# The second transposes of each binding part moved behind the part's weighted sums, in a four-layer transformer stack on one core

## What is computed

```python
x = x + attn_a(layernorm(x), qkvw, qkvb, ow, ob)
x = x + ffn(layernorm(x), weight, bias, centroids, assignments)
x = x + attn_b(layernorm(x), bv_q, bv_k, bv_v)
x = x + ffn(layernorm(x), weight, bias, centroids, assignments)

# attn_b: 4 heads of 256
scores = einsum('bthd,bshd->bhts', xh * q_bind, xh * k_bind) * scale
attn = where(causal, sigmoid(scores * 4.0), 0.0)
out = einsum('bhts,bshd->bthd', attn, xh * v_bind)

# ffn: x is (4096, 1024)
dots = softmax(x @ centroids.T / 0.1)
hits = dots > 0.01
out = where(any(hits, 1)[:, None] & any(hits, 0)[assignments][None, :], x @ weight.T + bias, 0)
```

## Time and profile before

| | |
|---|---|
| median of 3 runs | 3347.74 us (3346.71 to 3348.81) |
| the profiled execution, own time | 3343.6 us |
| its span in the trace | 3341.8 us |
| granted TensorE clock, mean over the span | 0.989 |
| TensorE busy | 3146.8 us (94%) |
| VectorE busy | 2271.2 us (68%) |
| GpSimd busy | 1940.3 us (58%) |
| ScalarE busy | 1744.6 us (52%) |
| first scores of steps 3 and 4 | 2647.66 and 2728.91 us |

### The profile page before, as it was taken

One profiled execution on the slowest core, in us unless ns is written; L12 is line 12 of the kernel. 1 busy time (PEld: TensorE's weight loads), 2 busy tenths in 40 slices (PEclk: granted clock), 3 DMA queues, 4 the chain that ended last, 5 costly groups with the idle time before them and its releaser, 6 DMA issues. The chain is left out here.

```text
span 3341.8 us, 62425 instructions
## 1 busy us (share of the span) xinstructions
PE 3146.8 (94%) x24128; PEld 1707.6 (51%) x24128; DVE 2271.2 (68%) x3919; ACT 1744.6 (52%) x2123; POOL 1940.3 (58%) x2065
## 2 busy tenths in 40 slices
PE   0899999999999999999989799998999999999999
PEld 0355555555555555555544455554455665655444
DVE  8377777777777777777877687776466666652622
ACT  3277777777777777777667522222245555552000
POOL 2277777777777777777666522221466666641522
PEclk9999999999999999999999899999999999999999
DMA  4122222222222222222334654453222323223643
GB/s 189 41 62 71 65 71 68 71 65 72 68 78 64 71 71 65 73 66 65 109 111 127 197 166 158 152 165 118 97 83 102 104 106 107 103 76 126 219 155 145
DMA packets 277927, 344.11 MB, mean 103 GB/s; under 512 B 92289, under 2 KB 206977, under 8 KB 276610
## 3 DMA queue, kind: packets, MB, share of 16 engines
q1 hardware_dynamic: 272962, 323.33, 30.6%
q10 hardware_dynamic: 4608, 16.78, 1.3%
q0 software_dynamic: 64, 0.01, 0.0%
HBM read 200.95 MB, written 138.55 MB: 102 GB/s over the span
## 5 line engine op out<-in xcount | busy, mean ns | idle before, releaser
L734 DVE TENSOR_REDUCE nmax<-ring_ps 128x1 f32<-128x512 f32 x1024 | 677.4, 687 | 417.0 <-PE ring_ps L535 414.5
L858 POOL TENSOR_TENSOR elo<-e,ehi 128x1024 f16<-128x1024 f32 x256 | 670.1, 2618 | 354.5 <-ACT ehi L671 354.5
L665 ACT ACTIVATE e<-st_ps,exp_scale 128x1024 f32<-128x1024 f32 x512 | 571.3, 1116 | 368.7 <-PE st_ps L545 307.6
L584 PE MATMUL proj_ps<-xnT,arena 128*128 128x512 f16 x3072 | 748.9, 380 | 3.3 <-DVE xnT L779 2.5
L671 ACT ACTIVATE ehi<-st_ps,exp_scale 128x1024 f16<-128x1024 f32 x512 | 569.0, 1111 | 0.0
L1587 PE MATMUL f_ps<-wT,fxT 128*128 128x512 f16 x1920 | 433.9, 381 | 2.9 <-DMA fxT<-xT_scratch 2.9
L584 PEld LDWEIGHTS proj_ps<-xnT,arena 128*128 128x128 f16 x3072 | 272.0, 97 | 285.9 <-ACT stage L683 11.8
L535 PE MATMUL ring_ps<-ks,qs 96*128 96x512 f16 x1024 | 396.0, 387 | 16.9 <-DVE nmax L734 16.1
L545 PE MATMUL st_ps<-qs,ks 98*128 98x512 f16 x1024 | 392.3, 383 | 12.5 <-ACT ehi L671 11.2
L562 PEld LDWEIGHTS ctx_ps<-v_sb,ehi 128*128 128x128 f16 x4096 | 312.2, 97 | 153.1 <-DVE sums L761 37.7
L562 PE MATMUL ctx_ps<-v_sb,ehi 128*128 128x65 f16 x4096 | 371.7, 192 | 13.3 <-DVE sums L761 11.8
(11 more groups left out here) (233 smaller groups left out, 4658.6 us busy)
## 6 DMA issues: line engine op xcount, KB each, us to landing
qk_scratch<-qk_hl SPq DMA_DIRECT2D x128, 256.0 KB, 2.3
fxT<-xT_scratch SPq DMA_DIRECT2D x64, 512.0 KB, 3.5
qs<-qk_scratch SPq DMA_DIRECT2D x192, 128.0 KB, 2.7
ks<-qk_scratch SPq DMA_DIRECT2D x192, 128.0 KB, 2.9
arena<-x_scratch SPq DMA_DIRECT2D x48, 512.0 KB, 4.4
ctx_scratch<-ctx SPq DMA_DIRECT2D x64, 256.0 KB, 3.2
xb<-in_L_attn_a_x_dram SPq DMA_DIRECT2D x32, 512.0 KB, 4.3
x_scratch<-xb SPq DMA_DIRECT2D x32, 512.0 KB, 2.6
```

The costliest lines, as they stand in the source:

```text
L584: mm = pe.matmul(proj_ps[:], wqk[:, wp, c, H * qk + P * g:H * qk + P * g + P], xnT[:, b % 2, xp, c, :], start=(n == 0), stop=(n == 23))
L665: nc.scalar.activation(e32[:, half], st_ps[:, half], ACT.Exp, scale=exp_scale[:, 0:1]).then_inc(e32_done, 1)
L734: dve.tensor_reduce(nmax[:, h % 2, c:c + 1], ring_ps[:, ring_max(h, c) % 2, :], AX.X, ALU.max, negate=True).then_inc(ring_free, 1)
L858: nc.gpsimd.tensor_tensor(elo[:, h % 2, 2:4, :], e32[:, 1], ehi[:, h % 2, 2:4, :], ALU.subtract).then_inc(elo_pool, 1)
```

## The change

In each part TensorE does the weighted sums of head hd before the second transposes of the tile of the batch before. The other queues keep their order.

```diff
                                 turn3(b - 1, hd, 0)
                                 ffn(b + 1, 4 + hd, 0, 24)
+                                weighted_b(b, hd)
                                 turn3(b - 1, hd, 1)
-                                weighted_b(b, hd)
```

## The result

The changed kernel takes 3372.17 us (median of 4 runs, 3371.99 to 3375.24) against 3347.69 us: 24.5 us more, ratio 1.0075, 95% interval 1.0058 to 1.0093. Forecast were 3369.1 us and a range of 3360 to 3380. The profiled execution took 3372.01 us.

What follows compares the result with a forecast made beforehand. TensorE's own work was taken to set the pace in the parts, the feeders at a step's start. 0.4 + 15.0 + 0 + 5.5 + 0.3 + 0.2 = 21.4 us on the 3347.7 median gave 3369.1 us, range 3360 to 3380.

Steps and rivals of the forecast that it cites:

- Parts 1 to 2 and 2 to 3: Steps 1 to 6: normalisations behind ScalarE's later copy make the first sigmoid 1.4 late; 12 x 1.25 = 15.0 us.
- the table load's row: At a step's start the table load holds the first sigmoid 1.30 us; the scores take 1.13 us longer.
- Part 0 to 1: First sigmoid in time; VectorE's and GpSimd's queues shift 2.47 us, yet the weighted sums do not wait: 0.
- The cover: Part 0 to 1: 0.36 us left between the scores' low halves and the weighted sums that need them.
- Part 3 to the next step: Bind products and casts come 2.7 late, 1.1 reaches the next start: 5.5 us over steps 1 to 5, then 0.3.
- Step 1: Part 0: weighted sums already wait for VectorE's low half, so the transposes come on top: +0.4 us, once.
- Step 7: One normalisation in place of two between parts, first sigmoid 0.3 us late, costing 0.1 twice: +0.2 us.
- Clock: Step starts idle 2.8 us; after 2.74 us at step 0 the clock stayed 1.00, so costed at nothing.
- The prediction's own sign against it: A clock below 1.00 in a steady step was listed as showing the forecast wrong, for rival 2's clock case.
- Rival 2's clock case: TensorE's clock falls after the longer waits at five step starts: 5 x 2.71 = 13.6 us more, 3383; chance 0.03.
- the feeders: Rival 1: step starts take up the delays, only the parts' 13.6 to 15.0 us remain: 3362; chance 0.10.
- the earlier weighted sums: Rival 4, faster: their earlier start reaches someone, at most step 1's 0.7 us wait: 3347; chance 0.01.

Runs made afterwards that it cites:

- e2: The new order in parts 1 and 2 of each step alone, against the kernel before: 3363.85 us, ratio 1.0046.
- e6: The kernel before with a one-column sigmoid in ScalarE's idle time, so that the table is loaded before the first scores: 3341.29 us, ratio 0.9982.
- e1: The new order in part 0 of each step alone, against the kernel before: 3348.10 against 3348.13 us, ratio 0.9997.
- e9: The changed kernel with VectorE's bind products ahead of its low half of the second transposes: 3363.05 against 3348.18 us before, ratio 1.0045.
- e5: The changed kernel with ScalarE's normalisations ahead of the copy (not in the last step) and VectorE's bind products ahead of its low half: 3347.98 against 3347.75 us before.
- e8: e5's order with the selection's exponentials moved to the eighth turn and the one-column sigmoid behind: 3347.32 us, ratio 1.0001 to the kernel before.
- e12: e8 with GpSimd's causal masks of part 0 ahead of one residual add: 3346.01 us, ratio 0.9992 to the kernel before.
- e3: The new order in part 3 of each step alone, against the kernel before: 3357.48 us, ratio 1.0028.
- e4: The changed kernel with ScalarE's normalisations ahead of its copy of the second transposes: 3361.50 us, ratio 1.0039 to the kernel before.
- e10: The changed kernel with the one-column sigmoid that loads the table early: 3370.33 us, ratio 1.0066 to the kernel before.
- e11: The kernel before with exponentials in the eighth turn, the early one-column sigmoid, and GpSimd's part 0 masks ahead of one residual add: 3343.38 against 3348.78 us.

## Why the prediction was right, point by point

- *Parts 1 to 2 and 2 to 3*, forecast 12 x 1.25 = 15.0 us: measured 12 x 1.24 = 14.9; e2 alone gives 15.1 with step 7's share. The late first sigmoid had its price in the table load's row; e6 shows that price going whole where the cause goes.
- *Part 0 to 1*, forecast 0: e1 shows +0.46 with step 1's 0.4 us in it. The cover is 0.36 us as worked out.
- *Part 3 to the next step*, forecast 1.1 each and 0.3 at step 7: the wait at a start grew from 1.68 to 2.79 (five times 1.1) and from 0.63 to 0.94 at step 7. That GpSimd's idle time takes up 1.6 of the 2.7 us was right: 1.1 arrive. e9 shows that it is VectorE's order alone that does it; ScalarE's late normalisation in part 3 has no share.
- *Step 1*, forecast 0.4: its wait is 1.13 in place of 0.70 us.
- *Step 7*, forecast 0.2: two waits of 0.12 us. The store and the loads on SP, costed at nothing, brought no wait.
- *Clock*, forecast 0: this is the step that was wrong. "I cost it at nothing" rested on one wait of 2.74 us at step 0 after which the clock stayed. It falls after some such waits and not after others. The prediction's own sign against it, a clock below 1.00 in a steady step, came. The falls in the changed kernel cost 0.64, 0.79, 1.06 and 1.28 us (first scores to first transposes less the 4.58 us of before), 3.8 in all. That is nearly the whole difference between the 21.4 us forecast and the 25.1 measured over the stretch; step 3 without its fall (0.79) takes 84.8 us as forecast. That the time lies in the stated range all the same is in part luck: the room above 3369 was there for a failing cover or a later start, not for the clock. Rival 2's clock case, with a chance of 0.03 and 13.6 us, had the mechanism, but its price, taken from 24 ffn products that all ran low, was too high (2.71 us against 1.5 to 1.7 for the scores at a start), and it had all five starts.
- The rivals: the feeders do not make up for the parts (e2); the late transposes cost only where something is queued behind them (e5); no one found a use for the earlier weighted sums (e5, e8).

The sum of the measured terms is 0.4 + 14.9 + 5.6 + 0.3 + 0.2 + 3.8 = 25.2 for 25.1 us.

## What to carry to other kernels

Moving an instruction on the engine that sets the pace moves everything that is queued behind its consumers on the others: price that list, engine by engine, and if the move is wanted, put the unrelated work of those queues ahead of the consumer (e5 took back about 24 us of 24.5). Small work that lies inside a wait is free; moved out of the wait, it has its price: in e8 and e12 the transposes' 0.43 us counted in every step in which the weighted sums wait. When a change lengthens a wait of TensorE, ask what the clock did after waits of that length in more than one place and more than one execution.

## What the runs showed of the hardware

- TensorE's clock after a wait. At the starts of steps 2 to 6, after waits of 2.78 to 2.83 us (the changed kernel, e3, e4, e10), the clock fell in 13 of 20; after waits of 1.67 to 1.70 us there (before, e1, e2, e5, e6, e9) in none of 30. In step 8 of e4 it fell after one of two waits of 2.59 us. At step 0, after 2.74 to 2.76 us, 24 scores took 5.1 to 5.3 us in eight profiled executions and 3.6 in six, among them the two of before and after. A fall seen alone costs 1.5 to 1.7 us over the 24 scores, and where the scores wait for the table load as well 0.6 to 1.3. The Trainium skill, "TensorE: Matmul & The Clock Gate", section "HAM oscillation — how this bites in real kernels", says that idle gaps send the clock down; the traces agree, with the addition that the same gap did so in some places and not in others. What decides between them is open.
- VectorE beside GpSimd: four subtractions with two SBUF inputs took 1.70 us alone and 2.78 us beside one GpSimd add of 1.27 us (e11), all of it on the first of the four.
